# Expert results of a Mamba and mixture-of-experts block: written to scratch and added up at the end, or added straight into the output rows

## The reference

```
h = layernorm(x) * (1 + cb) + sb                  # per token, cb and sb per sequence
scores = softmax(h @ gate_w.T)                    # 8 experts
top_vals, idx = top_k(scores, 2)                  # two experts for each token
xs = h * weight                                   # one scaled copy per chosen expert
y = sum over the two chosen experts e of
      (silu(xs @ w1[e].T + b1[e]) @ w2[e].T + b2[e]) * (xs @ w3[e].T + b3[e])
z = (silu(h @ sw1.T) * (h @ sw2.T)) @ sw3.T       # shared expert
out = x + gb * (y + z)                            # gb: one row of 256 numbers per sequence
```

## Time and profile before

| | |
|---|---|
| median of 3 runs | 2278.7 us |
| the profiled execution's own time | 2285.97 us |
| its span | 2284.2 us |
| mean granted TensorE clock | 0.846 |
| busy share over the whole span | VectorE 88%, TensorE 80%, GpSimd 80%, ScalarE 61% |

### The profile page before, as it was taken

The page is one execution under the profiler, slowest core; times in us unless marked ns, Lnnn a source line. Parts: engine busy times, 40 slices in busy tenths (PEclk is TensorE's granted clock), DMA queues, the critical chain, the costliest instruction groups (busy, mean ns, idle before and its releaser), DMA issues.

```text
span 2284.2 us, 23574 instructions
## 1 busy us (share of the span) xinstructions
PE 1821.2 (80%) x6088; PEld 758.2 (33%) x6089; DVE 2011.5 (88%) x2218; ACT 1384.1 (61%) x2412; POOL 1828.7 (80%) x719
## 2 busy tenths in 40 slices
PE   6687787978787978779787878787766599999992
PEld 3222232323232323323232323233221366655561
DVE  7799999999999999999999999999999767533335
ACT  4577768585767677685957676776755333423330
POOL 3399999989999999999999999999899433435551
PEclk9687887979797979789797879797866699999996
DMA  7734434343534344443434344443333351222226
GB/s 283 220 93 103 118 95 123 105 103 102 118 104 104 108 112 114 104 121 93 115 106 116 104 101 114 109 114 104 93 93 122 129 208 61 74 77 88 84 87 237
DMA packets 135966, 266.07 MB, mean 116 GB/s; under 512 B 20224, under 2 KB 39936, under 8 KB 134704
## 3 DMA queue, kind: packets, MB, share of 16 engines
q1 hardware_dynamic: 126448, 236.97, 38.5%
q0 software_dynamic: 6528, 17.87, 2.2%
q10 hardware_dynamic: 2880, 9.96, 1.1%
HBM read 198.62 MB, written 67.15 MB: 116 GB/s over the span
## 4 chain that ended last, share of the span: by engine, by line
DVE 43%; PE 25%; issue 15%; ACT 10%; POOL 4%; DMA 2%; SPq 1%; DVEq 0%; ACTq 0%; POOLq 0%
DVE hst L1302 29%; DVE dbu L1288 9%; PE psum L1890 6%; PE psum L1828 4%; ACT psum L1051 4%; PE psum L1910 3%; PE psum L1637 2%; POOL hst L785 2%; PE psum L1840 2%; PE psum L1703 2%; ACT L1051 1%; PE psum L1691 1%; ACT dt L1020 1%; DVE sz L1273 1%; ACT sp_tmp L1022 1%
## 5 line engine op out<-in xcount | busy, mean ns | idle before, releaser
L785 POOL TENSOR_TENSOR hst<-hst,c_rep 128x2048 f32<-128x2048 f32 x256 | 1155.7, 4531 | 67.7 <-DVE hst L1302 35.2
L1302 DVE TENSOR_TENSOR_SCAN hst<-psum,state,dbu 128x512 f32<-128x512 f32 x768 | 922.0, 1259 | 0.0
L1051 ACT ACTIVATE psum<-dt_rep,neg_a 128x512 f32<-128x512 f32 x1024 | 688.3, 683 | 374.5 <-DVE hst L1302 371.8
L1288 DVE TENSOR_TENSOR dbu<-psum,b_rep 128x2048 f32<-128x2048 f32 x192 | 435.0, 2266 | 16.0 <-PE psum L1691 10.2
L1691 PE MATMUL psum<-dt,same 32*128 32x512 f32 x384 | 258.8, 758 | 152.0 <-DVE dbu L1288 148.5
L1703 PE MATMUL psum<-hst,same 128*32 128x512 f32 x2048 | 304.5, 748 | 84.5 <-POOL hst L785 84.4
L774 POOL TENSOR_TENSOR dbu<-dtu_rep,b_rep 128x2048 f32<-128x2048 f32 x64 | 292.0, 4563 | 18.5 <-DVE hst L1302 17.7
L1302 DVE TENSOR_TENSOR_SCAN hst<-psum,dbu 128x512 f32<-128x512 f32 x256 | 291.6, 1198 | 1.1 <-ACT psum L1051 1.1
L1649 PE MATMUL psum<-xp,taps 128*128 128x512 f32 x512 | 238.6, 610 | 2.3 <-DVE sp_tmp L1281 1.1
L1637 PE MATMUL psum<-xnT,w_in 128*128 128x512 f32 x256 | 150.8, 719 | 47.3 <-ACT sz L983 47.3
L1703 PEld LDWEIGHTS psum<-hst,same 128*32 128x32 f32 x2048 | 71.0, 133 | 323.8 <-issue 199.2
(11 more groups left out here) (165 smaller groups left out, 2322.1 us busy)
## 6 DMA issues: line engine op xcount, KB each, us to landing
dt_rep<-dt_scratch SPq DMA_DIRECT2D x256, 256.0 KB, 4.7
taps<-taps_scratch SPq DMA_DIRECT2D x64, 256.0 KB, 2.9
b_rep<-bc_scratch SPq DMA_DIRECT2D x64, 256.0 KB, 4.8
c_rep<-bc_scratch SPq DMA_DIRECT2D x64, 256.0 KB, 7.8
dt_scratch<-dt SPq DMA_DIRECT2D x64, 256.0 KB, 2.0
dtu_rep<-dtu_scratch SPq DMA_DIRECT2D x256, 64.0 KB, 1.9
h<-slot_scratch SPq DMA_DIRECT2D x72, 128.5 KB, 2.1
sp_tmp<-t_scratch SPq DMA_DIRECT2D x16, 512.0 KB, 4.8
```

Source lines behind the costliest of these rows:

```text
L785: nc.gpsimd.tensor_tensor(h, h, c_rep[q % 2][:], ALU.mult).then_inc(prod_done, 1)
L1051: nc.scalar.activation(psum[:, PS_A + i, :], dt_rep[:, G % 2, j, :], ACT.Exp, scale=neg_a[:, q % 2, u, i:i + 1]).then_inc(exp_done, 1)
L1288: nc.vector.tensor_tensor(dbu[:, U % DBU, :, :], psum[:, PS_U:PS_U + 1, :].broadcast_to((P, NG, TB)), b_rep[U // UNITS % 2][:], ALU.mult). ...
L1302: nc.vector.tensor_tensor_scan(time_order(hst[:, U % RING, i, :], backward), time_order(psum[:, PS_A + i, :], backward), time_order(dbu[:, ...
```

## The change

The output tensor becomes `OUT_ROWS` rows of 256 numbers: 4096 token rows and 2048 trash rows. Once a block's shared part is in x1, SyncE stores the block's x1 to its output rows. In the tile loop the second half of `hx` is also multiplied by the gate gb of each row's sequence, and GpSimd's indirect store adds (`compute_op=ALU.add`) into the token's output row. Since a token's two rows are in different tiles, each accumulating store waits until the one before it has landed. The numbers that travel with the rows are token numbers in place of pair numbers. The pass at the end (loads, `finish`, stores) goes.

```
-        yout_dram = dram("yout_scratch", (PAIRS + 2 * NE * P, DM))
+        of_batch = sb3("of_batch", [P, UNROLL, BATCH])
+        row_gate = part(24, 2, 1)
# SyncE
+            sp.dma_start(out[TOKENS:OUT_ROWS].rearrange("(a p) d -> p a d", p=P), trash[:, :, 0:DM]
+                         ).then_inc(trash_kept, 16)
...
+            def store_block(p):
+                n = TAKEN[p]
+                sp.wait_ge(s_x1, 2 * p + 2)
+                sp.dma_start(out[n * TB:(n + 1) * TB].rearrange("(p t) d -> p t d", t=NT), x1[:, rows_of(n), :]
+                             ).then_inc(f_out, 16)
             for p in range(4, NBLK):
                 load_block(p)
+                store_block(p - 4)
+            store_block(NBLK - 4)
             sp.wait_ge(f_x1, 2 * NBLK)
             sp.dma_start(b2 ...).then_inc(f_w_loaded, 16)
+            store_block(NBLK - 3)
+            store_block(NBLK - 2)
...
-            sp.wait_ge(trash_kept, 16 * (2 + NE))
+            sp.wait_ge(trash_kept, 16 * (3 + NE))
             for s in range(4):
                 load_tile(s, s)
+            store_block(NBLK - 1)
...
-            for i in range(NBLK):          # 16 loads of yout_dram and 8 stores of x1, with their waits
-                ...
# GpSimd
+            pool.wait_ge(f_out, 16 * NBLK)
             def tiles(s, r):
+                pool.wait_ge(gated, s + 1)
                 pool.wait_ge(y_biased, s + 1)
                 nc.gpsimd.tensor_tensor(yt[:, r % 4, :], yt[:, r % 4, :], hx[:, r % 4, DM:2 * DM], ALU.mult
                                         ).then_inc(y_done, 1)
                 pool.wait_ge(y_done, s + 1)
+                if r > 0:
+                    pool.wait_ge(y_stored[(r - 1) % 4], (quarter(s - 1, r - 1) + 1) * 16)
+                elif not isinstance(s, int):
+                    pool.wait_ge(y_stored[3], quarter(s, r) * 16)
+                elif s > 0:
+                    pool.wait_ge(y_stored[3], s // 4 * 16)
                 wait_apart(pool)
                 nc.gpsimd.indirect_dma_start(
-                    yout_dram, bass.IndirectOffsetOnAxis(ap=target_u[:, r:r + 1], axis=0), yt[:, r % 4, :], None
-                    ).then_inc(y_stored[r % 4], 16)
+                    out, bass.IndirectOffsetOnAxis(ap=target_u[:, r:r + 1], axis=0), yt[:, r % 4, :], None,
+                    compute_op=ALU.add).then_inc(y_stored[r % 4], 16)
# ScalarE
                 if m == 0:
-                    act.wait_ge(trash_kept, 32)
+                    act.wait_ge(trash_kept, 48)
...
+            def begin_gate(s, r):          # last in ScalarE's tiles(s, r)
+                act.wait_ge(batch_known, 2 * s + 2)
+                if not (isinstance(s, int) and s < 2):
+                    act.wait_ge(gated, s - 1)
+                nc.scalar.activation(row_gate[:, r % 2, :], fmod[:, 0, 3, :], ACT.Copy, scale=of_batch[:, r, 0:1]
+                                     ).then_inc(gate_begun, 1)
# VectorE, in bias_hidden between L1540 and L1542
+                for b, op in enumerate((ALU.is_lt, ALU.is_ge)):
+                    nc.vector.tensor_scalar(of_batch[:, r, b:b + 1], xt[:, r % 4, DM:ROW], float(SEQ), None, op
+                                            ).then_inc(batch_known, 1)
...
+            def gate_rows(s, r):           # last in VectorE's tiles(s, r)
+                dve.wait_ge(gate_begun, s + 1)
+                dve.wait_ge(batch_known, 2 * s + 2)
+                nc.vector.scalar_tensor_tensor(row_gate[:, r % 2, :], fmod[:, 1, 3, :], of_batch[:, r, 1:2],
+                                               row_gate[:, r % 2, :], ALU.mult, ALU.add).then_inc(gate_done, 1)
+                dve.wait_ge(gate_done, s + 1)
+                dve.wait_ge(hx_done, s + 1)
+                nc.vector.tensor_tensor(hx[:, r % 4, DM:2 * DM], hx[:, r % 4, DM:2 * DM], row_gate[:, r % 2, :], ALU.mult
+                                        ).then_inc(gated, 1)
...
-            def finish(i):                 # L1561 to L1573, and its calls for 8 blocks
-                ...
```

More of the change, by code:

```diff
@@ L49 @@
 SPARE = NE * REGION
+TOKENS = BATCH * SEQ
+OUT_ROWS = TOKENS + 2 * NE * P
 ORDER = [0, 3, 1, 2, 4, 7, 5, 6]
@@ L217, in mixer_and_experts @@
         tile_no = sb3("tile_no", [P, TILES])
-        pair_i = sb3("pair_i", [P, 2, T3], I32)
-        pair_no = sb3("pair_no", [P, 2, T3])
+        token_i = sb3("token_i", [P, T3], I32)
+        token_no = sb3("token_no", [P, T3])
         trash_i = sb3("trash_i", [P, 2 * NE], I32)
@@ L415, in mixer_and_experts @@
         target_kept = sem("target_kept")
-        y_back = [sem(f"y_back{r}") for r in range(8)]
-        f_fin = sem("f_fin")
+        batch_known = sem("batch_known")
+        gate_begun = sem("gate_begun")
+        gate_done = sem("gate_done")
+        gated = sem("gated")
         f_out = sem("f_out")
@@ L674, in _ @@
                          ).then_inc(f_w_loaded, 16)
-            def store_block(i):
-                sp.wait_ge(f_fin, 3 * i + 3)
-                sp.dma_start(out[i], x1[:, i * NT:(i + 1) * NT, :].rearrange("p t d -> p (t d)")).then_inc(f_out, 16)
+            store_block(NBLK - 3)
+            store_block(NBLK - 2)
             def load_tile(s, r):
@@ L702, in _ @@
                 sp.wait_ge(y_stored[r], 16 * TILES // 4)
-            for i in range(NBLK):
[L704 to L715, removed]
             sp.wait_ge(f_out, 16 * NBLK)
@@ L796, in constants @@
                     nc.gpsimd.iota(count_i[:], pattern=[[1, TILES]], base=0, channel_multiplier=0).then_inc(f_count, 1)
-                    nc.gpsimd.iota(pair_i[:], pattern=[[BATCH * SEQ, 2], [P, T3]], base=0, channel_multiplier=1
+                    nc.gpsimd.iota(token_i[:], pattern=[[TB, NBLK], [1, NT]], base=0, channel_multiplier=NT
                                    ).then_inc(f_count, 1)
                 if t == 9:
-                    nc.gpsimd.iota(trash_i[:], pattern=[[P, 2 * NE]], base=PAIRS, channel_multiplier=1
+                    nc.gpsimd.iota(trash_i[:], pattern=[[P, 2 * NE]], base=TOKENS, channel_multiplier=1
                                    ).then_inc(f_count, 1)
@@ L812, in constants @@
                     nc.gpsimd.tensor_copy(tile_no[:], count_i[:]).then_inc(f_const, 1)
-                    nc.gpsimd.tensor_copy(pair_no[:], pair_i[:]).then_inc(f_const, 1)
+                    nc.gpsimd.tensor_copy(token_no[:], token_i[:]).then_inc(f_const, 1)
                 if t == 13:
@@ L1147, in scale_tokens @@
                                          ).then_inc(scaled, 1)
-                nc.scalar.activation(send[:, m % 4, :, DM], pair_no[:, k, rows_of(n)], ACT.Copy).then_inc(scaled, 1)
+                nc.scalar.activation(send[:, m % 4, :, DM], token_no[:, rows_of(n)], ACT.Copy).then_inc(scaled, 1)
             for n in range(NBLK):
@@ L1188, in tiles @@
                 silu_tile(s, r)
+                begin_gate(s, r)
             for r in range(4):
@@ L1555, in tiles @@
                     bias_result(s - 2, (r - 2) % UNROLL)
+                gate_rows(s, r)
             tile_loop(dve, tiles)
@@ L1559, in _ @@
             bias_result(TILES - 1, UNROLL - 1)
-            def finish(i):
[L1563 to L1576, removed]
         @block.tensor
@@ L1986 @@
            for name, v in arrays.items()}
-    out = nc.dram_tensor("out_x", (NBLK, P, NT * DM), F32, kind="ExternalOutput").ap()
+    out = nc.dram_tensor("out_x", (OUT_ROWS, DM), F32, kind="ExternalOutput").ap()
     mixer_and_experts(nc, aps, out)
@@ L1990 @@
     y = np.asarray(r.results[0]["out_x"])
-    return y.reshape(NBLK, P, NT, DM).transpose(0, 2, 1, 3).reshape(BATCH, SEQ, DM)
+    return y[:TOKENS].reshape(NBLK, P, NT, DM).transpose(0, 2, 1, 3).reshape(BATCH, SEQ, DM)
```

1 line of the change is left out of this document (removed).

## The result

The changed kernel takes 2366.51 us (median of 4 runs, 2364.57 to 2367.08) against 2280.51 us (4 runs, 2278.0 to 2283.48) for the kernel before: ratio 1.0363, 95% interval 1.035 to 1.0376. It is 3.6% slower. The prediction was 2328 with a range of 2269 to 2388: sign and mechanism held, the loss was larger than the likeliest value (86 us by the medians, 78.6 by the spans, 49.2 forecast).

A forecast was written before the change was run, and what follows sets the result against it. TensorE was taken to bound the tile loop at 3.04 us a tile; chained stores would make it 4.26. The loop loses 86.6 us, the tail returns 37.1: 49.2 net after roundings on 2278.7 gives 2328 us, range 2269 to 2388.

The forecast's parts named there:

- g: Tile loop: time from one store's landing to the next store's start, taken as 0.79 us between bounds 0.3 and 0.8.
- L: Tile loop: landing time of an accumulating store, 2.5 + 0.4 + 0.37 + 0.2 = 3.47 us; break-even at 2.79.
- its issue has more to say: Accumulating store on GpSimd: a longer issue adds 0.2 us to the landing, bounds nothing and 1.0 us.
- reading DRAM: Accumulating store: old rows must be read from DRAM before writing, adding 0.4 us to the landing.
- second stream: Accumulating store: a second stream of the same size through the 16 DMA engines adds 0.37 us, from 0 to 0.37.
- The tail: After the last store: of 41.0 us only one landing and 0.4 us remain, giving back 37.1 us.
- The other edits: Gating on VectorE and ScalarE, trash store, early output stores, GpSimd's first wait: all hidden, costing nothing.
- 1.5 us of slack at the new pace: Tile loop, VectorE: the added gating work is hidden by 1.5 us of slack per turn, against 0.3 at today's pace.
- the old rows' reading hides: Rival, chance 0.20: reading hides in the write's completion, landing 2.5 to 2.77 us; with 2.6, time 2265.
- second rival: Accumulating store, chance 0.08: one engine's rows go one after the other, landing 4.4 to 5.7 us; with 5.0, time 2438.
- TensorE's clock: Rival in the tile loop, chance 0.03: TensorE loses clock when idling a quarter of each turn; half clock gives 2458.
- The signs I had named: Loop: stores evenly spaced, preceding store ends GpSimd's idle, landing 3.1 to 4.0 us, TensorE near 70%; span ends one landing later.

The follow-up runs named there:

- the third experiment: The changed kernel with plain stores in place of accumulating ones, chain and gating kept: 2269.4 us, ratio 0.995 to the kernel before.
- the faster versions: The changed kernel waiting only between experts, GpSimd's product one tile ahead of its store: 2292.2 us; also without gating 2252.3 us, or with a cheaper gate 2253.5 us.

## Why the prediction was right, and where it was off

**The bound and the chain: right.** A turn is landing plus g. g was taken as 0.79 and is 0.78 as a rule, 0.82 in the mean. The formula for the span, 2083.6 + 72 L, gives 2363.0 with the mean landing of 3.88; the span was 2362.8. It comes this close in part by luck: 71 x 0.03 = 2 us more of g and 0.7 more at the end are set off by a first store that came 2.7 us earlier. The error is in L: 3.47 forecast, 3.88 measured, 0.41 us x 72 = 29.5 us, against 29.4 us between the forecast span (2333.4) and the real one. By the medians the miss is 38.5 us (2366.5 against 2328); the other 9 are that the profiled execution before lay 7.3 us above the median used and the one after 1.9 below its own.

**The terms of L.** The step that was mis-sized is "its issue has more to say": 0.2 us taken, 0.58 measured (1.584 against 1.007), which makes 0.38 x 72 = 27 us, nearly all of the miss in the span. The bounds had been 0 and 1.0, with no row between them, and I took a low value without a reason from a row. The other two terms, 0.4 for reading DRAM and 0.37 for the second stream, made 0.77, and measured is 3.88 - 1.58 = 2.3 us after the issue against 2.5 - 1.0 = 1.5, some 0.8.

The packets of single stores show where it lies. For the accumulating store at 2348.78 and the plain one of the third experiment at 2255.44, both after the last tile load, there is no packet until 2.14 and 1.57 us after the start. Then come all packets of the accumulating store (2350.92 to 2352.21), and of the plain one (2257.01 to 2257.54):

```profile
DMA packets 144, 0.13 MB, mean 102 GB/s; under 512 B 16, under 2 KB 144, under 8 KB 144
q0 software_dynamic: 144, 0.13, 96.9%
```

```profile
DMA packets 48, 0.13 MB, mean 247 GB/s; under 512 B 16, under 2 KB 16, under 8 KB 48
q0 software_dynamic: 48, 0.13, 69.1%
```

From the last packet to the landing it is 0.34 and 0.35 us. So of the 1.3 us that the landing grew by, 0.57 lie before the first packet, which is the longer issue, and 0.75 in the packets (1.27 against 0.52 us); nothing is added at the end. The plain store moves its rows in 32 large packets, the accumulating one in 128, one for each row, and keeps the 16 engines busy for 97% of that stretch. The other versions agree: half the rows has 64 such packets and half the width 128 of half the size. The reading and the "second stream" can't be told apart in them, and the profile counts the same 0.13 MB for both stores. The engines' time per store is also in the view of DMA queues (packets, MB, share of 16 engines) for the 200 us from 2040, with 43 stores after and 66 before; after, then before:

```profile
q0 software_dynamic: 6186, 5.64, 25.4%
```

```profile
q0 software_dynamic: 3151, 8.65, 12.3%
```

That is 0.254 x 200 / 43 = 1.18 us per store against 0.37, so the engines' part grew by 0.8, which is the forecast's 0.77 for both terms together. It is 0.64 us with half the rows and 0.77 with half the width.

**The tail: right.** With the landing that it took, 3.47 us, the prediction had the tail give back 37.1 us; from the last store's start to the end it is now 4.9 us instead of 41.0, 36.1 less. The plain-store experiment, which keeps the chain, has a span 18.7 us shorter than before (2265.5 against 2284.2): 37.4 us less behind its last store, 18.1 more in the loop and 0.6 at its start.

**The other edits.** The comparisons, gate row and product cost 7.5 to 13 us where nothing was forecast; the last output store (issued at 2013.13), the trash store and GpSimd's first wait delayed nothing: the first store started at 2024.4, 2.7 us earlier than before. The slack on VectorE that I counted, 0.3 us at TensorE's pace, did not exist. It left out two things that only the faster versions showed: half a microsecond per turn in which VectorE issues with no operation running, and the growth of its operations on SBUF beside GpSimd's product (484 to 899 ns). In the changed kernel the long turn covers the first, and the second hardly occurs, since the two seldom run at the same time (484 ns in the mean). With the product ahead the gating costs (3.61 - 3.06) x 71 = 39 us. "1.5 us of slack at the new pace" was what made the step come out right.

**The rivals.** That the old rows' reading hides (0.20) is refuted by the landing of 3.8. With it falls what I had derived beside it from the Trainium skill, DMA: Bandwidth & Descriptors, Anatomy of one DMA: an estimate of 2.6 us for twice the bytes. By that formula 128 KB of bytes are 0.3 us; this store's landing grew by 1.3. The same section of the Trainium skill, as the prediction says, puts most of the fixed part down to the write's receipt. The trace does not agree: here 0.34 to 0.35 us lie between the last packet and the landing, and 1.57 to 2.14 before the first packet.

Of the second rival (0.08) only the price is refuted: L would be 4.4 or more. Its picture was nearer than I gave it credit for. The store's row packets take 0.146 us in the mean, so 8 of them on each of 16 engines, one after the other, are 1.17 us, and the stretch with packets is 1.27 us long with the engines busy 97% of it. That is what rows one after the other would give, at 0.15 us each and not 0.4. TensorE's clock (0.03) stayed at 1.00 in every window from 2100 to 2340 us, though the engine idled a fifth of the time.

**The signs I had named.** Fairly even turns (4.5 to 4.9 us for eight in ten), a median landing within 3.1 to 4.0 us, TensorE well below 100% and an end right after the last store all came. One sign did not: the view of waits names VectorE before most stores. The chain of waits, and the version without gating, show that the landing ends these waits. TensorE was busy 80% and not 70%, though the turn was longer than forecast: its matmul records fill 3.8 us of a turn (48.2 of 60 us, turn 4.70) where they filled 3.04 before. Why is not shown.

## What to carry to other kernels

Before a transfer that nobody waits for is put on a chain, take its landing time plus the wake-up of the engine (here 0.8 us) and compare the sum with the loop's turn: 3.3 us against 3.04 already said that the wait costs something, and accumulation added 1.3 to 1.4 us to the landing. A hazard between two kinds of work needs a wait only where the kind changes: eight waits instead of 71 turned a loss of 3.6% into a gain of 1.4%, once GpSimd and VectorE had been relieved as well. When the bound moves away, the next engine's slack must be counted with its issue time between operations and with what runs beside it, not with the sum of its operations.

## What the runs showed of the hardware

- The indirect store of 128 rows of 1 KB takes GpSimd 1.007 us plain and 1.584 us accumulating; with 64 rows the accumulating one takes 1.438. The next product on GpSimd starts 1.03 us after the store in both and ends 0.76 us after the store's record ends, so its own record lasts 0.73 or 1.31 us.
- The accumulating store lands 3.8 us after its start against 2.4 to 2.6 plain. Its first packet comes 2.14 us after the start against 1.57, its packets take 1.27 us against 0.52, and the landing follows 0.34 to 0.35 us after the last one in both. It uses the 16 DMA engines for 1.18 us against 0.37, with 128 data packets against 32.
- A plain store landed in 2.4 to 2.5 us behind the last tile load, and in 2.69 us in the mean (2.4 to 3.5) where SyncE issued one within 0.6 us of its start (the version with only the wait).
- VectorE operations with both inputs in SBUF slow down beside GpSimd's product, and not beside its store: with the product ahead, the product with the gate takes 424 to 427 ns without it and 823 to 1382 ns with it; in the changed kernel 430 ns in the mean beside the store alone (64 times). Operations with an input in PSUM stayed at 691 and 425 ns beside either. How the two engines get in each other's way was not isolated.
